# 64-wide attention: two accumulation banks for the product with the values, two instead of three banks in the ring of projection rounds

## The reference

```
def _L1_xattn_ref(input_Q, input_K, input_V, Wq, bq, Wk, bk, Wv, bv, Wo):
    B, S, D, H, DK = (4, 512, 256, 16, 64)
    def _proj(x, W, b):
        y = jnp.einsum('bsd,ed->bse', x, W) + b
        return y.reshape(x.shape[0], x.shape[1], H, DK).transpose(0, 2, 1, 3)
    Q = _proj(input_Q, Wq, bq); K = _proj(input_K, Wk, bk); V = _proj(input_V, Wv, bv)
    scores = jnp.einsum('bhqd,bhkd->bhqk', Q, K) / np.sqrt(DK).astype(np.float32)
    attn = jax.nn.softmax(scores, axis=-1)
    context = jnp.einsum('bhqk,bhkd->bhqd', attn, V)
    context = context.transpose(0, 2, 1, 3).reshape(input_Q.shape[0], -1, H * DK)
    return jnp.einsum('bse,de->bsd', context, Wo)
...
x = x + _L1_xattn_ref(_layernorm(x, axis=-1), ctx_1024, ctx_1024, ...)
```

## Time and profile before

| | |
|---|---|
| median of three runs | 1708.25 us |
| profiled execution, its own time | 1712.9 us |
| its span | 1711.1 us |
| TensorE matmul busy in the span | 1440.0 us (84%) |
| VectorE busy | 1060.2 us (62%) |
| ScalarE busy | 829.6 us (48%) |
| the stage of the change | about 604 to 1024 us of the span |

### The profile page before, as it was taken

One profiled execution on the slowest core, in us unless ns is written; L12 is line 12 of the kernel. 1 busy time (PEld: TensorE's weight loads), 2 busy tenths in 40 slices (PEclk: granted clock), 3 DMA queues, 4 the chain that ended last, 5 costly groups with the idle time before them and its releaser, 6 DMA issues. The chain is left out here.

```text
span 1711.1 us, 28961 instructions
## 1 busy us (share of the span) xinstructions
PE 1440.0 (84%) x9522; PEld 1153.9 (67%) x9522; DVE 1060.2 (62%) x2423; ACT 829.6 (48%) x1944; POOL 488.4 (29%) x426
## 2 busy tenths in 40 slices
PE   3799874999999759999999984899667995888885
PEld 3566542888888657888888862799555884655553
DVE  4677634566666537666667756444387645597776
ACT  1366642444544337666667753355325451455441
POOL 2111011477777600000000004455212302134343
PEclk9899966999999979999999996799898996699887
DMA  4322125356556356544455422122262002221110
GB/s 127 114 87 89 59 75 197 108 130 163 140 130 165 61 129 143 129 120 114 111 135 139 108 96 102 49 76 78 87 213 68 1 0 69 70 78 63 62 47 25
DMA packets 139973, 169.30 MB, mean 99 GB/s; under 512 B 20000, under 2 KB 131616, under 8 KB 137312
## 3 DMA queue, kind: packets, MB, share of 16 engines
q1 hardware_dynamic: 115504, 132.34, 26.2%
q0 software_dynamic: 16032, 27.01, 7.3%
q10 hardware_dynamic: 8336, 8.65, 1.6%
HBM read 76.18 MB, written 24.12 MB: 59 GB/s over the span
## 5 line engine op out<-in xcount | busy, mean ns | idle before, releaser
L904 DVE TENSOR_REDUCE a_nmax<-a_s 128x2 f32<-128x512 f32 x256 | 171.1, 685 | 109.4 <-PE a_s L819 108.8
L1090 ACT ACTIVATE a_probT<-a_t 128x512 f32<-128x512 f32 x256 | 151.7, 601 | 177.3 <-PE a_t L823 151.7
L63 POOL TENSOR_TENSOR a_rstd<-a_veps,minus_half 128x2 f32<-128x2 f32 x32 | 22.8, 714 | 560.2 <-DVE a_veps L57 560.2
L819 PE MATMUL a_s<-a_ka,a_qa 48*128 48x256 f32 x512 | 125.2, 348 | 45.2 <-DVE a_nmax L904 21.4
L819 PEld LDWEIGHTS a_s<-a_ka,a_qa 48*128 48x128 f32 x512 | 80.4, 207 | 107.0 <-issue 61.9
L432 DVE TENSOR_REDUCE a_nmax<-a_score 128x2 f32<-128x512 f32 x128 | 88.2, 689 | 103.4 <-PE a_score L329 101.0
L1609 POOL DMA_INDIRECT x_rows<-f_hn,f_scatter_row x60 | 129.8, 2164 | 16.4 <-issue 16.4
L515 ACT ACTIVATE a_prob<-a_score,a_nmax 128x256 f32<-128x256 f32 x256 | 120.4, 482 | 23.7 <-DVE a_nmax L432 23.0
L823 PE MATMUL a_t<-a_qa,a_ka 50*128 50x256 f32 x512 | 125.7, 345 | 2.2 <-DMA a_qa<-a_m_lo 1.2
L524 ACT COPY a_probT<-a_T 128x512 f32<-128x512 f32 x128 | 76.0, 595 | 75.7 <-PE a_T L337 74.1
L1552 ACT ACTIVATE f_gate<-f_gate 128x512 f32<-128x512 f32 x64 | 38.3, 599 | 128.5 <-PE f_gate L1355 110.5
(11 more groups left out here) (374 smaller groups left out, 4344.6 us busy)
## 6 DMA issues: line engine op xcount, KB each, us to landing
area_odd<-in_L_experts SPq DMA_DIRECT2D x15, 1536.0 KB, 6.9
a_k_hi<-a_k_fresh_hi SPq DMA_DIRECT2D x128, 128.0 KB, 2.4
a_ctxT<-in_ctxT SPq DMA_DIRECT2D x64, 128.0 KB, 2.6
a_ka<-a_k_hi SPq DMA_DIRECT2D x128, 64.0 KB, 2.6
a_qa<-a_q_hi SPq DMA_DIRECT2D x128, 64.0 KB, 2.6
a_k_lo<-a_k_fresh_lo SPq DMA_DIRECT2D x64, 128.0 KB, 2.4
a_q<-a_q_fresh_hi SPq DMA_DIRECT2D x64, 128.0 KB, 2.4
a_q<-a_q_fresh_lo SPq DMA_DIRECT2D x64, 128.0 KB, 2.4
```

The source lines that it names most:

```text
L819: last_s = nc.tensor.matmul(ps_s[i][:, half, :], qa[rows, u % RING, j, half * P:(half + 1) * P], ka[rows, u % RING, j, :], start=True, sto ...
L904: nc.vector.tensor_reduce(nmax[:, u % 2, :, i * PPU + j], ps_s[i][:, :, :], AX.X, ALU.max, negate=True).then_inc(sem["nmax"], 1)
L1090: nc.scalar.activation(probT[:, t % NPT, i, :, :], ps_t[i][:, :, :], ACT.Exp).then_inc(sem["exp"], 1)
```

## The change

`NPB` goes from 3 to 2: the ring has two banks, and round r waits for round r - 2 instead of r - 3. `OUT` stays 1, but bank 1 now holds the rounds 1, 3, 5, 7, 9 and 11, and `held` becomes v2. The bank set free becomes a second `ps_o`; the chunks use the two in turn, and `weighted_values(c)` waits for the copy of chunk c - 2 instead of c - 1. In batch 0, round v2 moves from step 3 to step 4, beside v3.

```
-    NPB = 3
+    NPB = 2
...
-    FIRST_STEP = {("k", 1): 0, ("q", 1): 0, ("v", 0): 1, ("k", 2): 1, ("v", 1): 2, ("q", 2): 2, ("k", 3): 3, ("q", 3): 3, ("v", 2): 3, ("v", 3): 4}
+    FIRST_STEP = {("k", 1): 0, ("q", 1): 0, ("v", 0): 1, ("k", 2): 1, ("v", 1): 2, ("q", 2): 2, ("k", 3): 3, ("q", 3): 3, ("v", 2): 4, ("v", 3): 4}
...
-        ps_o = pb("o", [P, S])
+        ps_o = [pb(f"o{i}", [P, S]) for i in range(2)]
...
-                   "stats aggr veps rstd hn zeros proj0 proj1 proj2 out ctx ctx_hi ctx_lo hT_hi hT_lo k_hi k_lo "
+                   "stats aggr veps rstd hn zeros proj0 proj1 out ctx ctx_hi ctx_lo hT_hi hT_lo k_hi k_lo "
...
-        proj = (sem["proj0"], sem["proj1"], sem["proj2"])
+        proj = (sem["proj0"], sem["proj1"])
...
-                after(pe, sem["oT"], b * NCH + c)
+                after(pe, sem["oT"], b * NCH + c - 1)
...
-                        last = nc.tensor.matmul(ps_o[i * HD:(i + 1) * HD, :], vb[:, kc, at:at + HD], probT[:, c % 2, kc, i, :],
+                        last = nc.tensor.matmul(ps_o[c % 2][i * HD:(i + 1) * HD, :], vb[:, kc, at:at + HD], probT[:, c % 2, kc, i, :],
...
-                nc.scalar.copy(oT[:, c, :, :], ps_o[:, :].rearrange("p (q s) -> p q s", q=TB)).then_inc(sem["oT"], 1)
+                nc.scalar.copy(oT[:, c, :, :], ps_o[c % 2][:, :].rearrange("p (q s) -> p q s", q=TB)).then_inc(sem["oT"], 1)
```

## The result

The changed kernel takes 1717.6 us (median of 8 runs, 1711.5 to 1720.1), the kernel before 1705.2 us in the same measurement: a ratio of 1.007 with a 95% interval of 1.0047 to 1.0092, that is 8.0 to 15.7 us more. The prediction said 9.9 us more and 1718.2 us. That 1718.2 lies so near to 1717.6 is in part luck: it stands on the median of the first three runs of the kernel before, which was 3.0 us above the median of all eight, and the difference itself came out 2.5 us larger than forecast. The profiled executions stand at 1718.3 and 1711.1 us of span, but spans also differ by what other stages did. The cleaner measure is the stage itself, from its first transpose to the start of its last addition: 1030.92 - 602.60 = 428.3 us after, 1023.38 - 605.27 = 418.1 us before, 10.2 us more.

The account below looks back on a forecast made before the run. TensorE, busy 49.33 of 50 us, was taken to bound the stage. Terms 0 + 0 + 8.4 + 1.5 = 9.9 us on the median 1708.25 gave 1718.2 us, range 1710 to 1724 us.

Parts of the forecast that it names:

- The second accumulation bank: Products with the values, line 348: the copy's wait is met long before it is reached, so 0 us gained.
- The rival that would have made the change free: Line 348: the copy's wait causes the idle time there, so 10.7 us gained, 1707.5 us in all; chance 0.05.
- The ring in the running batches: Rounds waiting for the round before the last: tightest slacks 1.22 us at v2 and 1.07 us at hT; cost 0.
- the ring of two stalls in every batch: Running batches: a slack of 1.07 us becomes a wait of about 1 us, 7 us more, 1725.2 us; chance 0.06.
- the slack of 1.07 us at hT: Round hT starts at 797.95 and needs v3, read by 796.88; the slack holds when the whole batch moves.
- The output's wait: Step 4, batches 1 to 7: output waits 1.10 us for VectorE's reading of v2, plus 0.10 us restart; 8.4 us.
- the wait costs nothing: Output projection: its wait doesn't slow the batches and only batch 0 pays, 1709.8 us; chance 0.08.
- Batch 0: Packed rounds: early delays end in an existing DMA wait; v2 now needs k3, so v3 follows later; 1.5 us.
- The clock: Batch 0: new gaps drop TensorE's clock to 1.2 GHz for five rounds, 5.4 us, 1723.6 us; chance 0.08.

Follow-up runs that it names:

- Experiment 1: Changed kernel without the second accumulation bank, so the ring of two alone: ratio 1.0046 to the kernel before, stage 429.1 us, pass 50.62 us.
- experiment 3: Changed kernel with round v3 made ahead of the output projection in step 4: ratio 1.0002 to the kernel before, stage 420.0 us, pass 49.40 us.
- experiments 1 and 4: The second of these: ring of two, one accumulation bank, the freed bank for the output alone, which waits for no round: ratio 1.0027 to the kernel before.
- experiment 2: Kernel before with three banks, its output projection waiting for the reading of v2 instead of q3: ratio 1.0051, stage 428.6 us, pass 50.62 us.
- experiment 5: Changed kernel with VectorE reading v2 ahead of the maximum of step 4: ratio 1.0011 to the kernel before, stage 423.7 us, pass 50.00 us.
- the first run of experiment 6: Kernel before, unchanged, profiled again (first repetition): stage 420.0 us, the scores of step 7 at 46.92 us.

## Why the prediction was right

**The second accumulation bank, 0 us: right.** Experiment 1 leaves it out and changes neither the pass nor the idle time at line 348. The rival that would have made the change free is refuted.

**The ring in the running batches, 0 us: right.** The pass is 49.40 us with a ring of two once the output doesn't wait (experiment 3). The rival "the ring of two stalls in every batch" is out, and the slack of 1.07 us at hT held. But it was not the smallest. I had read the slacks from the third pass of the loop. In step 12 of batch 0, where TensorE makes the v0 of batch 1, the trace of the kernel before has k1 read by 664.69 + 0.87 = 665.56 and v0 starting at 665.69, 0.13 us later. A ring of two makes v0 wait for that reading, and the reading waits for DMAs. In the changed kernel it just fitted (0.27 us to spare); in experiments 1 and 4 it did not (0.5 us each).

**The output's wait, 7 x 1.20 = 8.4 us: right, and shown by itself.** The pass grew by 1.20 us; experiment 2 makes the same 1.2 us with three banks, and experiment 5 takes 0.60 us off by VectorE's order alone. The rival "the wait costs nothing" is out.

**Batch 0, 1.5 us: the size nearly right (1.66), the way to it only in part.** I had let all delays end in the wait for k2's DMAs, with 2 us to spare, and took it that these DMAs would land when they did before. They did not: ScalarE read k3 at 639.73, 37.13 us into the stage, against 643.53 - 605.27 = 38.26. That is no chance of one execution. The last of k2's copies took 2.4 us from issue to landing in all seven traces with a ring of two and 3.7 to 4.2 us in all seven with three banks, though it was issued at the same time, 34.3 to 34.7 us into the stage. What differs beside it is q2: its copies followed 0.65 us behind with three banks and 0.9 to 1.1 us with two, because q2 now waits for k2. That they slowed each other is an argument from these rows; no run shows it by itself. So what came last was TensorE's own work. The scores of step 4 started at 640.31, VectorE's maximum and its reading of k3 followed, and v2 started at 642.51. So the waits of v0, v1 and k3 did reach the end, and it is a coincidence that this cost what late DMAs would have. v2 and v3 one after the other then took 3.31 us and not 2.98, because v3 had to wait 0.3 us for q3.

**The clock: the rival had the wrong kernel.** I feared that more gaps in batch 0 would let the clock fall in the changed kernel. In seven traces with a ring of two it never fell there. It fell in five of seven with three banks: after waits for k3 of 2.5 to 2.9 us, and not after the waits of 2.20 and 2.40 us. The change breaks this wait up, and no piece was longer than 1.6 us. That the pieces are the reason is argued from these rows; no run changed the wait's length and nothing else. The two forms bear on the cost: the four traces of the kernel before have a mean stage of 419.2 us, 1.1 us above the first one, from which the 10.2 us are counted.

**The total.** 10.2 us in the stage, less this 1.1 us, is 9.1 us, inside the measured 8.0 to 15.7 us. The rest of the middle value, 12.4 us, I can't place: outside this stage the spans of single executions differ by up to 20 us (1293.0 us before, 1272.9 us in the first run of experiment 6) under identical code.

## What to carry to other kernels

When a ring of buffers gets shorter, don't only count steps between a round and its successor in the ring. Look for the guest that uses the ring out of turn, here the output projection: its predecessor is now another round, read one step later, and the price is set by that read and by what stands ahead of it in the reader's order. Look also at the slacks at the edges of the loop and not in one pass of it alone. Such a wait can be covered by moving one independent round ahead of it. A second buffer is worth nothing where no wait for the first is in the profile. And a stage's own length, from its first to its last instruction, tells more than the kernel's time: over four executions of the kernel before it differed by 1.9 us, where eight runs of the changed kernel differed by 8.6 us.

## What the runs showed of the hardware

The granted clock can differ between executions of one program at the same place. In batch 0 of the kernel before and of its variants with three banks, TensorE waits for k3 for 2.2 to 2.9 us, depending on when the placing DMAs land. After the longer of these waits (2.5 us and more) the clock went from 2.4 to 1.2 GHz for a few us, at a cost of some 1.5 us; after the shorter ones (2.20 and 2.40 us) it stayed up. The waits of 0.9 to 1.6 us in batch 0 of the seven traces with a ring of two never did that, though there are five of them within 20 us. Copies of one size can differ by half and more in their time to land: the last of k2's copies (128 KB) took 2.4 us when the next ones were issued 0.9 to 1.1 us after it, and 3.7 to 4.2 us when they were issued 0.65 us after it.
